# Two layers of graph attention on one core: gather indices, padding and score halves are read from where they are kept, and the copies go

## The chip, the cores and the metric

The kernel runs on one core of one Trainium2 chip. The metric is device time of that core in microseconds. The median of three runs of the kernel before is 1991.99 us (1989.11 to 1997.27). The engines are named as the profile names them: PE (matrix products), DVE (vector), ACT (activations), POOL (here the issuer of the row gathers) and SP (the issuer of the plain transfers).

## The reference

The input is x, 8192 nodes by 128 features, and adj, a matrix of 8192 by 8192 int32 in which about 9 entries a row are set. Two layers follow each other.

```
h = relu(layernorm(x))
# layer 0: scores from two projections
h0 = h @ W;  e = leaky_relu((h0 @ a1)[:, None] + (h0 @ a2)[None, :], 0.2)
x  = x + elu(softmax(where(adj > 0, e, -9e15)) @ h0)
h = relu(layernorm(x))
# layer 1: scores from query and key
q, k, v = h @ Wq.T + bq, h @ Wk.T + bk, h @ Wv.T + bv
x  = x + elu(softmax(where(adj > 0, q @ k.T / sqrt(128), -9e15)) @ v)
```

Since so few entries of a row are set, the kernel lists each row's neighbours once, gathers their rows and computes softmax over these alone. If a list overflows, a whole other branch does the full computation; for these inputs it isn't taken.

## The kernel before, in words

The 8192 rows are 64 tiles of 128 rows, one row a partition. All engines run a fully unrolled pipeline; the order of work on each is the order in which it is written, and semaphores join them.

**Layer 0, `survey`.** Step t of the loop works on several tiles at once. SP has loaded 4 MB of adj for a tile in four quarters; ACT turns each quarter into a BF16 mask (L1180), PE packs the mask into words in PSUM by 16 products of 512 columns (L1358), DVE pulls the largest words out (L701, L756 to L763, `decode` in every second step) and so gets up to 24 neighbours a row: 6 regular ones in the row's own list, and 18 more ("over") that are dealt among 384 places, 3 chunks of 128. For tile t-3 `mark` (L790, L793) says which places are whose, PE deals the lists out to them (L1422), ACT copies the result to `owned_list` (L1229), and `pick` makes the nine columns of indices, the padding and the part of the scores that is the row's own. POOL then issues nine gathers for the tile, 128 rows of a table each (L574), one column of indices each. For tile t-6 `score0`, `maxima`, `below` compute the scores (L847, L849, L841, L854 to L858, L862), for tile t-7 the rows are weighed and summed (L868, L875, L878, PE L1405, L891) and `finish` writes X.

The loop that joins the engines in a step: DVE L862 (`below`, waits for PE's L1398), then `pick`, `finish` and L868 on DVE, then PE L1405, L1391 and L1422, then ACT L1229 and two more quarters of the mask, then PE's L1358, and the next L862.

**Layer 1, `attend`.** The lists are kept, one entry a tile: `idx_all` (indices), `slot_all`, `pad_all` (padding, BF16), `end_all`, `pre_all`. Step t: `publish` copies the next tile's indices from `idx_all` to `idx_now` (four buffers) and tells POOL by `idx_done` (L1106), `prepare` rebuilds `hot`, `mine` and copies the padding to F32 (L1112 to L1118), `score1` computes the products with the gathered rows (L1129, L1132, L1135), `add_slots` sums (L883, L886). POOL issues nine gathers a tile (L604). There are four buffers `Gt` of gathered rows, so the gathers of tile t wait until `total` (L891) has finished tile t-4.

What the change touches is `pick` (L810 to L834), `score0` (L847), `maxima` (L854, L856), `publish` (L1106), `prepare` (L1113) and POOL's two gather loops.

## Time and profile before

| what | us |
|---|---|
| median of three runs | 1991.99 |
| profiled execution, its own time | 2002.33 |
| its span | 2000.6 |
| DVE busy / POOL busy / PE busy | 1361.0 / 1204.1 / 1256.1 |
| ACT busy | 772.2 |
| stretch 200 to 1040 us: layer 0 in its regular pace | 840 |
| stretch 1100 to 1950 us: layer 1 | 850 |

"Busy" counts the time in which an engine executes something; instructions that follow each other closely overlap in the records, so an instruction's duration can be longer than the distance to the next one's start. "<-" names who ended a wait; "remote" is a release that the profile can't put down to an instruction.

### The profile page before, as it was taken

The page shows a single profiled execution, that of the slowest core. Times are in us where ns is not written, and L with a number is a line of the kernel's source. Part 1 is how long each engine was busy: PE and PEld are TensorE (multiplying, and loading weights), DVE is VectorE, ACT ScalarE, POOL GpSimd, SP SyncE. Part 2 cuts the span into 40 slices and gives each one's busy share as a digit, 9 for nine tenths or more (in the row PEclk, how much of TensorE's full clock was granted, in tenths as well). Part 3 has the DMA queues.
Part 4 walks back from the last instruction along what each step waited for, and adds up shares of the span by engine and source line. Part 5 has one row for each costly group of instructions (what it writes and reads, how often), then busy time and mean ns, then how long its engine had stood idle before and what let it go on. Part 6 is the DMA issues. An engine that isn't in the chain of part 4 may idle for free.

```text
span 2000.6 us, 21643 instructions
## 1 busy us (share of the span) xinstructions
PE 1256.1 (63%) x5314; PEld 974.4 (49%) x5362; DVE 1361.0 (68%) x5505; ACT 772.2 (39%) x1507; POOL 1204.1 (60%) x1206
## 2 busy tenths in 40 slices
PE   2756677666776767776654345676766475838466
PEld 1433444444444444544444345575665475738355
DVE  4565777777777777777776356786776485838467
ACT  2774566565666666565631111121111111201111
POOL 1345555555555555555565566777777777757773
PEclk9886776766667666676765556655555555555666
DMA  9788999999999999989822111222222222212121
GB/s 311 272 310 322 326 318 330 336 310 325 316 334 321 330 310 332 331 320 329 313 55 48 50 45 49 58 54 57 53 57 54 54 55 57 54 44 60 49 56 40
DMA packets 122251, 372.31 MB, mean 186 GB/s; under 512 B 34577, under 2 KB 67858, under 8 KB 89362
## 3 DMA queue, kind: packets, MB, share of 16 engines
q1 hardware_dynamic: 75458, 289.83, 39.5%
q0 software_dynamic: 38464, 81.08, 15.7%
q10 hardware_dynamic: 8208, 0.03, 0.2%
q8 instruction: 46, 0.75, 0.2%
q14 instruction: 75, 0.61, 0.1%
HBM read 358.12 MB, written 12.72 MB: 185 GB/s over the span
## 4 chain that ended last, share of the span: by engine, by line
DVE 50%; another core or an unknown queue 19%; issue 12%; PE 10%; ACT 4%; POOL 2%; DMA 1%; SPq 1%; DVEq 0%; ACTq 0%; POOLq 0%
DVE arena L875 5%; DVE arena L701 3%; DVE arena L760 3%; DVE arena L763 3%; DVE arena L886 3%; ACT arena L1180 3%; DVE arena L1135 2%; POOL arena L604 2%; DVE arena L793 2%; DVE arena L868 2%; DVE arena L883 2%; DVE arena L1129 2%; PE psum L1398 1%; PE psum L1405 1%
## 5 line engine op out<-in xcount | busy, mean ns | idle before, releaser
L574 POOL DMA_INDIRECT arena<-table,arena x576 | 549.7, 954 | 424.1 <-DVE arena L829 262.2
L604 POOL DMA_INDIRECT arena<-table,arena x576 | 626.1, 1087 | 238.6 <-issue 171.0
L1180 ACT ACTIVATE arena<-arena 128x2048 bf16<-128x2048 int32 x256 | 485.4, 1897 | 26.2 <-DMA arena<-in_adj_dram 26.0
L1405 PE MATMUL psum<-arena 128*128 128x131 f32 (+1 forms) x768 | 206.2, 439 | 398.8 <-DVE arena L868 251.3
L1358 PE MATMUL psum<-arena 128*128 128x512 bf16 x976 | 334.9, 488 | 102.1 <-ACT arena L1180 55.2
L1405 PEld LDWEIGHTS psum<-arena 128*128 128x128 f32 x768 | 172.0, 322 | 414.0 <-issue 413.5
L1358 PEld LDWEIGHTS psum<-arena 128*128 128x128 bf16 x1024 | 117.6, 125 | 273.5 <-issue 169.0
L1315 ACT ACTIVATE arena<-psum 128x384 f32<-128x384 f32 x64 | 31.5, 492 | 437.9 <-PE psum L1525 202.0
L862 DVE TENSOR_TENSOR arena<-arena,psum 128x3 f32<-128x3 f32 x128 | 19.6, 153 | 260.6 <-remote 196.0
L1391 PEld LDWEIGHTS psum<-arena 128*128 128x128 f32 x768 | 161.6, 303 | 28.4 <-issue 15.6
L1391 PE MATMUL psum<-arena 128*128 128x18 f32 x768 | 152.7, 334 | 25.7 <-issue 14.2
L1398 PEld LDWEIGHTS psum<-arena 128*128 128x128 f32 x768 | 143.6, 264 | 50.5 <-issue 26.6
L1398 PE MATMUL psum<-arena 128*128 128x1 f32 x768 | 132.8, 288 | 32.1 <-issue 16.9
L1229 ACT ACTIVATE arena<-psum 128x465 f32<-128x465 f32 x64 | 35.7, 558 | 282.3 <-PE psum L1422 154.6
L875 DVE SCALAR_TENSOR_TENSOR arena<-arena 128x131 f32<-128x131 f32 x384 | 130.6, 340 | 6.5 <-DVE arena L878 2.0
L1211 ACT ACTIVATE arena<-arena 128x3 f32<-128x3 f32 x128 | 26.2, 205 | 273.5 <-DVE arena L862 160.5
L1422 PE MATMUL psum<-arena 128*128 128x155 f32 x384 | 120.8, 486 | 2.9 <-issue 1.4
L1524 PE MATMUL psum<-arena 128*128 128x128 f32 x384 | 120.0, 415 | 1.0 <-DVE arena L1123 1.0
L1525 PE MATMUL psum<-arena 128*128 128x129 f32 x384 | 117.5, 406 | 0.0
L886 DVE TENSOR_REDUCE arena<-arena 128x129 f32<-128x903 f32 x64 | 111.9, 1748 | 2.2
L1535 PE MATMUL psum<-arena 128*128 128x128 f32 x128 | 44.5, 445 | 103.6 <-ACT arena L1322 80.3
L856 DVE TENSOR_TENSOR arena<-psum,arena 128x18 f32<-128x18 f32 x128 | 21.9, 171 | 124.8 <-remote 122.6
(201 smaller groups left out, 2396.2 us busy)
## 6 DMA issues: line engine op xcount, KB each, us to landing
arena<-in_adj_dram SPq DMA_DIRECT2D x256, 1024.0 KB
arena<-table,arena POOLq DMA_INDIRECT x1152
table<-arena POOLq DMA_DIRECT2D x32, 132.0 KB, 5.3
arena<-table SPq DMA_DIRECT2D x64, 66.0 KB
table<-arena SPq DMA_DIRECT2D x16, 256.0 KB
arena<-table SPq DMA_DIRECT2D x64, 64.0 KB
out_dram<-arena SPq DMA_DIRECT2D x16, 256.0 KB
arena<-in_x_dram SPq DMA_DIRECT2D x4, 0.5 KB, 12.1
```

What stands on the lines that cost most here:

```text
L574: pool.indirect_dma_start(Gt[:, v % GROUP, c + 1, :], None, table0, bass.IndirectOffsetOnAxis(idx_now[:, v % GROUP, c:c + 1], 0))\
L604: pool.indirect_dma_start(Gt[:, t % GROUP, c + 1, 0:D], None, table1, bass.IndirectOffsetOnAxis(idx_now[:, t % GROUP, c:c + 1], 0))\
L875: nc.vector.scalar_tensor_tensor(out=acc_sb[:, k, 0:width], in0=Gt[:, r, c, 0:width], scalar=p10[:, k, c:c + 1], in1=acc_sb[:, k, 0:width] ...
L886: nc.vector.tensor_reduce(acc_sb[:, k, 0:DE], slots.rearrange("p c d -> p d c"), AX.X, ALU.add).then_inc(chained, 1)
L1180: nc.scalar.activation(mask[:, k, q * QUARTER:(q + 1) * QUARTER], adj_sb[:, k, q, :], ACT.Relu, accum_out=sum_all[:, bass.ds(tile, 1), q:q ...
L1358: nc.tensor.matmul(V[k], shifted[:, s, :], mask[:, k, s * 512:(s + 1) * 512], start=(s == 0), stop=False)
L1391: last = nc.tensor.matmul(by_slot_ps[k], owned[:, r, c, :], slot_e[:, k, c, :], start=(c == 0), stop=(c == CHUNKS - 1))
L1398: last = nc.tensor.matmul(max_ps[k][:, c:c + 1], mine[:, r, c * P:(c + 1) * P], neg_max[:, k, :], start=True, stop=True)
L1405: last = nc.tensor.matmul(acc_ps[k][:, 0:width], weighted[:, c, :], Gt[:, r, OWN + c, 0:width], start=(c == 0), stop=(c == CHUNKS - 1))
L1422: last = nc.tensor.matmul(deal_ps[v % 2][:, c, :], mine[:, v % GROUP, c * P:(c + 1) * P], dealt[:, v % GROUP, :], start=True, stop=True)
L1524: nc.tensor.matmul(own_ps[m][:, c, :], mine_c, ident[:, :], start=True, stop=True)
L1525: last = nc.tensor.matmul(uq_ps[m][:, c, :], mine_c, u_row[:, j, P:], start=True, stop=True)
```

## The change

`pick` writes its indices straight into the tile's entry of `idx_all` and its padding straight into `pad_all`; the F32 copy of the padding (`pad`), the four-buffered `idx_now` and the ten scores' own half (`s1_10`) are no longer there. POOL's gathers of both layers read `idx_all`. In layer 1 POOL no longer waits for `idx_done`, and `publish` and the copy of the padding are gone. `maxima` adds the BF16 padding. `score0` adds the own half in two instructions in place of one: seven columns with the row's own value from `self_s1` as scalar, three with what was dealt in `owned_list`. A tile of layer 0 has four DVE instructions less in `pick` and one more in `score0`; a tile of layer 1 has two less.

```diff
@@ gpsimd, layer 0 and layer 1 @@
-                                            bass.IndirectOffsetOnAxis(idx_now[:, v % GROUP, c:c + 1], 0))\
+                                            bass.IndirectOffsetOnAxis(idx_all[:, v, c:c + 1], 0))\
...
                     pool.wait_ge(summed, T + t - 3)
-                    pool.wait_ge(idx_done, T + t + 1)
...
-                                                bass.IndirectOffsetOnAxis(idx_now[:, t % GROUP, c:c + 1], 0))\
+                                                bass.IndirectOffsetOnAxis(idx_all[:, t, c:c + 1], 0))\
@@ pick @@
-            PICK_STEPS = 10
+            PICK_STEPS = 6
...
-                nc.vector.tensor_copy(s1_10[:, b, OWN:ROWS], ps[:, :, DEALT - 1]).then_inc(pick_done, 1)
+                nc.vector.tensor_scalar(idx_all[:, v, 0:REGULAR], dealt[:, b, LISTED:over], 0.0, float(N), ALU.max, ALU.min)\
+                  .then_inc(pick_done, 1)
                 after(1)
...
-                nc.vector.tensor_scalar(idx_now[:, b, 0:REGULAR], dealt[:, b, LISTED:over], 0.0, float(N), ALU.max, ALU.min)\
-                  .then_inc(pick_done, 1)
                 after(3)
...
-                nc.vector.tensor_scalar(s1_10[:, b, 0:OWN], ones[:, 0:OWN], dealt[:, b, DEALT - 1:DEALT], None, ALU.mult)\
-                  .then_inc(pick_done, 1)
-                after(5)
-                nc.vector.tensor_reduce(node_q[:, :], picked[:, :, :], AX.X, ALU.add).then_inc(pick_done, 1)
-                nc.vector.tensor_scalar(pad[:, b, :], dealt[:, b, P:LISTED + SLOTS], 0.0, NEG, ALU.is_le, ALU.mult)\
-                  .then_inc(pick_done, 1)
-                after(7)
-                nc.vector.tensor_scalar(idx_now[:, b, REGULAR:], node_q[:, :], 0.0, float(N), ALU.max, ALU.min)\
-                  .then_inc(idx_done, 1)
                 nc.vector.tensor_scalar(pad_all[:, at, :], one(dealt[:, b, P:LISTED + SLOTS]), 0.0, NEG, ALU.is_le, ALU.mult)\
                   .then_inc(pick_done, 1)
-                dve.wait_ge(idx_done, v + 1)
-                nc.vector.tensor_copy(idx_all[:, at, :], idx_now[:, b:b + 1, :]).then_inc(pick_done, 1)
+                after(4)
+                nc.vector.tensor_reduce(node_q[:, :], picked[:, :, :], AX.X, ALU.add).then_inc(pick_done, 1)
+                after(6)
+                nc.vector.tensor_scalar(idx_all[:, v, REGULAR:], node_q[:, :], 0.0, float(N), ALU.max, ALU.min)\
+                  .then_inc(idx_done, 1)
@@ score0 @@
-                nc.vector.tensor_tensor(e10[:, :], Gt[:, r, :, D], s1_10[:, r, :], ALU.add).then_inc(e_done, 1)
-                dve.wait_ge(e_done, u + 1)
+                nc.vector.tensor_scalar(e10[:, 0:OWN], Gt[:, r, 0:OWN, D], self_s1[:, u, 1:2], None, ALU.add).then_inc(e_done, 1)
+                nc.vector.tensor_tensor(e10[:, OWN:ROWS], Gt[:, r, OWN:ROWS, D], owned_list[:, r, :, DEALT - 1], ALU.add)\
+                  .then_inc(e_done, 1)
+                dve.wait_ge(e_done, 2 * u + 2)
@@ maxima @@
-                nc.vector.tensor_tensor(S[:, k, 0:OWN], l10[:, k, 0:OWN], pad[:, r, 0:OWN], ALU.add).then_inc(s_done, 1)
+                nc.vector.tensor_tensor(S[:, k, 0:OWN], l10[:, k, 0:OWN], pad_all[:, tt % T, 0:OWN], ALU.add).then_inc(s_done, 1)
...
-                nc.vector.tensor_tensor(S[:, k, OWN:], by_slot_ps[k], pad[:, r, OWN:], ALU.add).then_inc(s_done, 1)
+                nc.vector.tensor_tensor(S[:, k, OWN:], by_slot_ps[k], pad_all[:, tt % T, OWN:], ALU.add).then_inc(s_done, 1)
@@ prepare, attend @@
-                def publish(t, b):
-
-                    nc.vector.tensor_copy(idx_now[:, b:b + 1, :], idx_all[:, bass.ds(t, 1), :]).then_inc(idx_done, 1)
...
-                    nc.vector.tensor_scalar(pad[:, b:b + 1, :], pad_all[:, at, :], 1.0, None, ALU.mult).then_inc(hot_done, 1)
```

On DVE, `pick` of one tile in layer 0 before, from `below` (L862) to `finish` (L900):

```order
L862 TENSOR_TENSOR arena<-arena,psum 128x3 [waits max_spread]
L810 TENSOR_TENSOR arena<-arena 128x3 [waits owned_done]
L812 COPY arena<-arena 128x3
L814 TENSOR_TENSOR arena<-arena 128x54 [waits pick_done]
L817 TENSOR_SCALAR arena<-arena 128x6
L820 TENSOR_TENSOR arena<-arena 128x54 [waits pick_done]
L822 TENSOR_SCALAR arena<-arena 128x7
L825 TENSOR_REDUCE arena<-arena 128x3 [waits pick_done]
L826 TENSOR_SCALAR arena<-arena 128x25
L829 TENSOR_SCALAR arena<-arena 128x3 [waits pick_done]
L831 TENSOR_SCALAR arena<-arena 128x25
L834 COPY arena<-arena 128x9 [waits idx_done]
```

And the same place of the changed kernel (its line numbers differ; L853 is `below`):

```order
L853 TENSOR_TENSOR arena<-arena,psum 128x3 [waits max_spread]
L806 TENSOR_TENSOR arena<-arena 128x3 [waits owned_done]
L808 TENSOR_SCALAR arena<-arena 128x6
L811 TENSOR_TENSOR arena<-arena 128x54 [waits pick_done]
L815 TENSOR_TENSOR arena<-arena 128x54 [waits pick_done]
L817 TENSOR_SCALAR arena<-arena 128x25
L820 TENSOR_REDUCE arena<-arena 128x3 [waits pick_done]
L822 TENSOR_SCALAR arena<-arena 128x3 [waits pick_done]
```

The copy of the dealt half, the own half, the F32 padding and the last copy are gone; the six regular indices stand where the first copy stood, and two instructions now follow directly the one that they wait for.

On DVE, a step of layer 1 before, from `total` (L891) to `weigh` (L868):

```order
L891 TENSOR_TENSOR arena<-psum,arena 128x129 [waits chained,acc_done]
L894 RECIPROCAL arena<-arena 128x1 [waits summed]
L1112 TENSOR_SCALAR arena<-arena 128x384 [waits mine_done]
L1113 TENSOR_SCALAR arena<-arena 128x25
L1114 TENSOR_TENSOR arena<-arena 128x54
L1118 SCALAR_TENSOR_TENSOR arena<-arena 128x384 [waits fe_done]
L862 TENSOR_TENSOR arena<-arena,psum 128x3 [waits max_spread]
L900 SCALAR_TENSOR_TENSOR arena<-arena 128x128 [waits post_done,x_done]
L903 SCALAR_TENSOR_TENSOR arena<-arena 128x128 [waits y_done]
L1106 COPY arena<-arena 128x9
L868 TENSOR_TENSOR arena<-arena 128x384 [waits owned_done,p_done]
```

And of the changed kernel:

```order
L882 TENSOR_TENSOR arena<-psum,arena 128x129 [waits chained,acc_done]
L885 RECIPROCAL arena<-arena 128x1 [waits summed]
L1099 TENSOR_SCALAR arena<-arena 128x384 [waits mine_done]
L1100 TENSOR_TENSOR arena<-arena 128x54
L1104 SCALAR_TENSOR_TENSOR arena<-arena 128x384 [waits fe_done]
L853 TENSOR_TENSOR arena<-arena,psum 128x3 [waits max_spread]
L891 SCALAR_TENSOR_TENSOR arena<-arena 128x128 [waits post_done,x_done]
L894 SCALAR_TENSOR_TENSOR arena<-arena 128x128 [waits y_done]
L859 TENSOR_TENSOR arena<-arena 128x384 [waits owned_done,p_done]
```

The copy of the padding between L1112 and L1114 is gone, and so is `publish` ahead of `weigh`.

## Rows read from the trace of the kernel before

**Rows 1.** The page, busy time of each engine.
```profile
PE 1256.1 (63%) x5314; PEld 974.4 (49%) x5362; DVE 1361.0 (68%) x5505; ACT 772.2 (39%) x1507; POOL 1204.1 (60%) x1206
```
**Rows 2.** Waits, 200 to 1040 us: us in total, times, longest.
```profile
DVE arena L862 <- remote: 99.4, 28, 4.6
...
POOL arena L574 <- DVE arena L829: 226.8, 54, 4.9
```
**Rows 3.** Waits, 1100 to 1950 us: us in total, times, longest.
```profile
DVE arena L856 <- remote: 114.1, 19, 15.8
DVE arena L862 <- remote: 96.7, 13, 20.0
...
POOL arena L604 <- DVE arena L891: 58.9, 14, 13.3
```
**Rows 4.** Timeline, DVE in layer 0: start, us, instruction.
```profile
598.29 0.16 DVE L862 TENSOR_TENSOR arena<-arena,psum 128x3 f32<-128x3 f32 x1 [4.52 <-remote]
598.36 0.16 DVE L810 TENSOR_TENSOR arena<-arena 128x3 f32<-128x3 f32 x1
598.44 0.16 DVE L812 COPY arena<-arena 128x3 f32<-128x3 f32 x1
598.55 0.21 DVE L814 TENSOR_TENSOR arena<-arena 128x54 f32<-128x54 f32 x1
...
598.80 0.22 DVE L820 TENSOR_TENSOR arena<-arena 128x54 f32<-128x54 f32 x1
...
599.31 0.17 DVE L829 TENSOR_SCALAR arena<-arena 128x3 uint32<-128x3 f32 x1
599.38 0.17 DVE L831 TENSOR_SCALAR arena<-arena 128x25 bf16<-128x25 f32 x1
...
599.60 0.29 DVE L900 SCALAR_TENSOR_TENSOR arena<-arena 128x128 f32<-128x128 f32 x1
...
601.92 0.17 DVE L847 TENSOR_TENSOR arena<-arena 128x10 f32<-128x10 f32 x1
602.12 0.17 DVE L849 SCALAR_TENSOR_TENSOR arena<-arena 128x10 f32<-128x10 f32 x1
```
**Rows 5.** Timeline, the loop through PE and ACT after the next steps.
```profile
613.86 0.14 DVE L862 TENSOR_TENSOR arena<-arena,psum 128x3 f32<-128x3 f32 x1
...
617.80 1.65 PE L1405 MATMUL psum<-arena 128*128 128x131 f32 x6 [3.81 <-DVE arena L868]
...
622.97 0.56 ACT L1229 ACTIVATE arena<-psum 128x465 f32<-128x465 f32 x1 [4.52 <-PE psum L1422]
...
628.82 0.16 DVE L862 TENSOR_TENSOR arena<-arena,psum 128x3 f32<-128x3 f32 x1 [3.32 <-remote]
```
**Rows 6.** Groups of DVE instructions: xcount, busy, mean ns.
```profile
L822 DVE TENSOR_SCALAR arena<-arena 128x7 f32<-128x7 f32 x64 | 14.4, 225 | 0.0
...
L1113 DVE TENSOR_SCALAR arena<-arena 128x25 f32<-128x25 bf16 x64 | 11.4, 178 | 0.0
L1106 DVE COPY arena<-arena 128x9 uint32<-128x9 uint32 x64 | 11.3, 178 | 0.0
L826 DVE TENSOR_SCALAR arena<-arena 128x25 f32<-128x25 f32 x64 | 11.3, 176 | 0.0
...
L834 DVE COPY arena<-arena 128x9 uint32<-128x9 uint32 x64 | 11.0, 172 | 0.5 <-DVE arena L829 0.5
```
**Rows 7.** The page, gathers of layer 1: busy, mean ns, idle before.
```profile
L604 POOL DMA_INDIRECT arena<-table,arena x576 | 626.1, 1087 | 238.6 <-issue 171.0
```
**Rows 8.** Timeline, a `publish`, the gather beside it and the one before.
```profile
1524.26 0.94 POOL L604 DMA_INDIRECT arena<-table,arena  x1 [0.30 <-issue]
1525.51 0.98 POOL L604 DMA_INDIRECT arena<-table,arena  x1 [0.30 <-issue]
...
1525.92 0.17 DVE L1106 COPY arena<-arena 128x9 uint32<-128x9 uint32 x1
1525.99 0.55 DVE L868 TENSOR_TENSOR arena<-arena 128x384 f32<-128x384 f32 x1
```

More of the change, by code:

```diff
@@ L124, in two_layer_graph_attention @@
         hot = place([GROUP, CHUNKS, OVER])
-        pad = place([GROUP, 1 + SLOTS])
-        idx_now = place([GROUP, ROWS - 1], U32)
         owned_list = place([GROUP, CHUNKS, DEALT])
@@ L190, in two_layer_graph_attention @@
         e10 = place([ROWS])
-        s1_10 = place([GROUP, ROWS])
         picked = place([CHUNKS, OVER])
@@ L1133, in score1 @@
                       .then_inc(e_done, 1)
-                    dve.wait_ge(e_done, T + 2 * u + 2)
+                    dve.wait_ge(e_done, 2 * T + 2 * u + 2)
                     nc.vector.tensor_reduce(l10[:, k, :], prod[:, :, :], AX.X, ALU.add).then_inc(score_done, 1)
@@ L1142, in attend @@
                         back, m = (b - 3) % GROUP, (b - 3) % 2
-                        if live(t, -1):
-                            publish(t + 1, (b + 1) % GROUP)
                         if live(t, 3):
@@ L1165, in _ @@
                 dve.wait_ge(dve_consts, DVE_CONSTS + 3)
-                publish(0, 0)
                 unrolled(attend, G + 1)
```

## The prediction

> **What bounds the kernel now.** I read the busy times first, then the waits of each engine in the two regular stretches, then the timeline of a few steps. No engine is full: DVE, the busiest, has 68% of the span [rows 1]. So the time is in the loops that join the engines, and a removed instruction is worth what it shortens the loop in which it stands.
>
> Layer 0 has a pace of two steps. DVE starts L862 at 598.29, 613.86 and 628.82 us: 15.57 us and then 14.96 us [rows 4, 5]. Ahead of the first and the third it had waited, 4.52 and 3.32 us; ahead of the second it hadn't [rows 4, 5]. So one step of a pair (with `decode`) is DVE's own length, and the other is closed by the way through L868, PE, ACT and PE's L1398: L862 at 613.86, PE L1405 at 617.80, ACT L1229 at 622.97, L862 at 628.82 [rows 5]. The waits of the whole stretch say the same: 28 waits of L862, 99.4 us, none over 4.6, in 28 pairs of steps [rows 2]. The release is called "remote", so what exactly ends that wait the profile doesn't say. POOL isn't in this loop: it waited 226.8 us for the indices in the same stretch [rows 2].
>
> Layer 1 is less plain. DVE waits 114.1 us before L856 and 96.7 before L862, 32 times, "remote" again [rows 3]; POOL has 626.1 us of gathers and 171.0 of gaps between them, together 797 us, and waits for DVE's L891 only 58.9 us, 856 with it [rows 3, 7]: that is the length of layer 1 (the stretch of 850 us and its edges). So POOL is nearly full there, and a faster DVE can give at most those 58.9 us unless it makes the gathers shorter.
>
> **The change, part by part.**
>
> *`pick`.* Four instructions go: the copy L812, the own half L822, one of the two paddings (L826, L831) and the copy L834. L812 lasts 0.16 us [rows 4], the others 225, 176 and 172 ns [rows 6], 0.73 us together. But they overlap with their neighbours: L810, L812, L814 start 0.08 and 0.11 us apart [rows 4], and most of the removed ones fill the time in which a dependent instruction waits for its input. From L810 to L900 it now takes 598.36 to 599.60, 1.24 us [rows 4]. What is left is a chain: L814, then L820, the sum, the last three indices. L814 to L820 takes 0.25 us with a filler between; L814's 0.21 and the 0.03 that a dependent instruction adds (L847 lasts 0.17 and L849 starts 0.20 later, with nothing between) give 0.24 without [rows 4]. So the fillers inside the chain go for nothing, and the chain ends at 0.95 us as before (L810 to L829, [rows 4]). What is saved is its tail: L831 and L834 between L829 and L900, 0.29 us now [rows 4], of which 0.08 stays as the distance of two neighbours. That is 0.21 us a tile. The gathers see their indices at the same time as before; POOL's slack of 226.8 us covers them in any case [rows 2].
>
> *`score0`.* One instruction becomes two. The second starts 0.08 us after the first by the nearest row (L810 to L812), and the wait of L849 is for the later one: 0.08 us a tile more. Its upper end is a full duration and the wait, 0.20 us (L847 to L849) [rows 4]. This stands behind L868, so it lengthens DVE's own step, and not the part from L862 to L868.
>
> *`maxima`* reads the padding in BF16 beside F32. No row has just that; the nearest is L1113 with a BF16 input, 178 ns, against L826 with F32, 176 [rows 6]. Nothing, between -0.01 and +0.01 us a tile.
>
> *Layer 1.* `publish` goes: L1106 to L868 is 0.07 us [rows 8], and L868 is what PE waits for, so it stands in every step's loop. The copy L1113 lasts 178 ns [rows 6] but costs a distance of 0.08, and behind it DVE often waits at L862 anyway: between 0 and 0.08 us, I take 0.02. POOL's wait for `idx_done` ended nothing: all its waits were for L891 [rows 3]; 0. The gather beside a `publish` took 0.98 us [rows 8], and I count at most 0.04 us a tile for it, since a neighbour in the same shadow (L868) may be the cause.
>
> **The sum.** In layer 0 a pair of steps saves 0.21 in the step closed through PE and ACT and 0.21 - 0.08 = 0.13 in the one that is DVE's own, 0.34 us. Of the 32 pairs some 30 run at the regular pace (28 stand in the stretch alone, [rows 2]): 10.2 us. The other ends: 30 x 0.13 = 3.9, less the upper price of `score0` (0.12 more a tile, 7 us), so -3 us at worst; and 37 us if full durations counted (below). In layer 1, 64 x 0.09 = 5.8 us on DVE. Since POOL is nearly full, I take the half that its waits let through and a little for shorter gathers: 3.4 us; the ends are 0 and 64 x (0.15 + 0.04) = 12. Together 13.6 us. The profiled execution took 2002.33 us, 1.7 more than its span and 10.3 above the median; 2002.33 - 13.6 = 1988.7, which is 0.68% less, and on the median 1991.99 that is 1978.5. I say 1979.
>
> **Rules weighed.** The distances in rows 4 say that a small instruction costs 0.07 to 0.13 us where nothing waits on it. The Trainium skill ("VectorE: DVE Perf Modes", section "The TRN2 errata") says instead that instructions reading SBUF pay a fixed extra latency each, exposed between instructions. By that rule each removed instruction gives its whole length back, which is rival C; the starts 0.08 us apart speak against it.
>
> The gather beside a copy took 0.98 us, the one before it, with no copy beside it, 0.94 [rows 8]. The Trainium skill ("SBUF — State Buffer", section "Who interferes with whom") says that a copy or `tensor_scalar` in a 2-port mode takes a port pair that DVE shares with GpSimd and shuts it out for the whole instruction. By that rule POOL would win each removed copy in full, which is rival D.
>
> **The rivals.**
>
> B, hidden (chance 0.27): what ends the "remote" wait ahead of L862 isn't fed by L868 but by ACT's masks, whose pace is that of the adj loads. Then L868's earlier start ends in a longer wait, and only the DVE-owned steps shorten: 30 x 0.13 = 3.9 us, and layer 1, kept by POOL, gives 2. For it: the release has no name, and ACT reads the next quarters in the same loop. Against it: ACT L1229 waited 4.52 us for PE [rows 5], so ACT had time. Time: 1992 - 6 = 1986.
>
> C, full durations (0.03): 0.73 - 0.15 (L810's kind for the new one) = 0.58 us a tile, 37 us in layer 0, and 64 x (0.178 + 0.178) = 23 in layer 1: 1932.
>
> D, gathers set free (0.06): in layer 1 the two removed copies gave POOL back 0.178 us each a tile, 23 us there, with the 10 of layer 0: 1959. For it: POOL is the fuller engine there. Against it: a publish lasts 0.17 and the gather beside it grew by 0.04.
>
> E, slower (0.09): layer 1's "remote" stalls. They are 32 with 210.8 us, 6.6 us each [rows 3], and come after runs of short steps, when DVE has gained on POOL. A shorter DVE step can make such a run end sooner and bring another stall. Three more would cost 20 us against the 13.6 gained, +6; from three it decides, and with four it is +13: 2005. For it: layer 1's steps aren't regular, so small shifts are passed on. Against it: the sum of the stalls should stay what POOL's pace leaves over.
>
> **How the numbers follow.** My own case has the remaining 0.55, with a range of 1972 to 1986 (the ends of `score0` and of layer 1). Within 0.5% is about what a measurement of this kernel can't tell from no change; that is 1982 to 2002. About three quarters of my case lie below 1982, 0.42, with C and D 0.51, and a little of B: 0.53 faster. Same: the rest of my case, most of B and a third of E: 0.39. Slower: 0.08. The range of 8 in 10 reaches from 1964, halfway to D, to 1994, over B and up to where E begins.
>
> **What would show it.** In the profile after: L810's successor to L900's, 1.03 us instead of 1.24; the two steps of a pair at 15.44 and 14.75 us in place of 15.57 and 14.96; the waits of L862 in layer 0 nearly as long as now. If the 14.96 stays and the wait of L862 grows by 0.2 us each, B is right. If the step falls by over 0.5 us, C. In layer 1 the mean gather is to stay at 1.08 us or so; under 1.05 is D. POOL's wait for `total` should fall by a few us. The stalls before `maxima`'s second part and `below` should sum to about 200 us; over 230 is E. I am wrong if layer 0's stretch doesn't shorten by 7 us or more.

## The result: 4.3% slower, and where the time went

The changed kernel took 2069.57 us (median of 4 runs, 2062.02 to 2085.15) against 1990.55 beside it (4 runs, 1987.24 to 1997.27): ratio 1.0428, 95% interval 1.0388 to 1.0468 (the two medians alone give 1.040). The forecast was 1979. Ratios in this document are of fast runs: a run over 1.5% above the fastest of its kernel is left out of them, though not of the medians. The profiled execution took 2072.7 us, its span is 2071.0.

The page's busy times, with the columns of [rows 1]:
```profile
PE 1246.6 (60%) x5362; PEld 968.4 (47%) x5362; DVE 1335.0 (64%) x5185; ACT 773.2 (37%) x1507; POOL 1202.9 (58%) x1206
```
DVE has 320 instructions and 26 us less, and the span is 70.4 us longer. From the first `below` to the 64th (L862 before, L853 now) layer 0 took 940.2 us and takes 1014.8; layer 1 took 840.2 and takes 845.5. So the loss is in layer 0. The waits of its regular stretch, 200 to 1040 us, which answer [rows 2] (us in total, times, longest; POOL is GpSimd):
```profile
POOL arena L571 <- DVE arena L822: 240.6, 39, 14.7
...
DVE arena L780 <- remote: 97.0, 10, 11.1
...
DVE arena L853 <- remote: 58.8, 26, 4.4
...
DVE arena L780 <- issue: 19.8, 2, 9.9
```
A wait is there that before hardly had: DVE before L780, the first instruction of `split`, 12 times with 117 us (its counterpart L784 waited 2.8 us in all). `split` waits for PE's `ends` matmul, which is last of its step on PE. The starts of L853 show the pattern: groups of 14.8, 14.8, 12.1 and 24.7 us (66.4) where before had mostly 15.0 and 15.6 in turn (60.2 to 61.4 for four, 60.9 in the mean of 13 groups). In the two groups without a long step they are 14.8, 14.9, 14.8, 15.5: 60.0 us.

One long step on DVE, with start and duration, the wait ahead of it in brackets:
```profile
567.47 0.17 DVE L822 TENSOR_SCALAR arena<-arena 128x3 uint32<-128x3 f32 x1
567.55 0.29 DVE L891 SCALAR_TENSOR_TENSOR arena<-arena 128x128 f32<-128x128 f32 x1
...
570.71 0.56 DVE L859 TENSOR_TENSOR arena<-arena 128x384 f32<-128x384 f32 x1
581.16 0.16 DVE L780 TENSOR_TENSOR arena<-psum,arena 128x2 f32<-128x2 f32 x1 [9.89 <-issue]
```
On PE the same time reads as if the step's last matmuls had been done by 568.2:
```profile
564.12 0.72 PE L1381 MATMUL psum<-arena 128*128 128x1 f32 x6
...
567.66 0.39 PE L1348 MATMUL psum<-arena 1*128 1x512 bf16 x1
567.98 0.18 PE L1426 MATMUL psum<-arena 128*128 128x2 bf16 x1
571.48 1.65 PE L1388 MATMUL psum<-arena 128*128 128x131 f32 x6 [3.33 <-DVE arena L859]
582.33 1.47 PE L1374 MATMUL psum<-arena 128*128 128x18 f32 x6 [9.19 <-DVE arena L830]
```
The ends of matmuls are modelled. The semaphore events in the same trace are not, and they say otherwise: L1348's signal (`packed`) came at 580.43, 12.4 us after its recorded end, and L1388's at 581.92, not 573.1. GpSimd meanwhile ran two tiles' gathers through, with 0.79 us between them where 4 us are usual:
```profile
566.69 0.94 POOL L571 DMA_INDIRECT arena<-table,arena  x1 [0.30 <-issue]
568.43 0.95 POOL L571 DMA_INDIRECT arena<-table,arena  x1 [0.79 <-issue]
...
578.64 0.94 POOL L571 DMA_INDIRECT arena<-table,arena  x1 [0.30 <-issue]
```
From here on I read each PE signal by its lag, the semaphore event less the recorded end. I call a signal with a long lag held. Some events are missing from a trace, and such a signal then shows the next one's; a lag of about a step's length or more is such a case. Lags of `spread_max` (PE L1398 before, L1381 now), the signal that `below` waits for, from 200 to 1040 us:

| kernel | signals | lag under 0.3 us | 0.3 to 2 | over 2 |
|---|---|---|---|---|
| before | 55 | 0 | 0 | 55 |
| after | 50 | 12 | 9 | 29 |

Of the 21 early ones of the changed kernel, 10 came while their tile's gathers still ran, and the other 11, with 0.01 us, are those of the long steps, after the hold.

And in the trace of before, 53 of the 55 signals came 1.6 to 2.2 us (median 2.0) after the end of GpSimd's last gather of the tile, whatever PE had done by then. Here is one, GpSimd, then DVE:
```profile
564.75 0.94 POOL L574 DMA_INDIRECT arena<-table,arena  x1 [0.30 <-issue]
569.77 0.94 POOL L574 DMA_INDIRECT arena<-table,arena  x1 [4.08 <-DVE arena L829]
```
```profile
567.78 0.16 DVE L862 TENSOR_TENSOR arena<-arena,psum 128x3 f32<-128x3 f32 x1 [2.77 <-remote]
```
Last gather ends 565.69, signal 567.76, L862 at 567.78, next gather 569.77. That was the loop of the kernel before: nine gathers (8 x 1.25 + 0.94 = 10.95 us), 2.0 us to PE's signal, 2.0 us over `below` and `pick` to the next gather, 15.0 us. The "remote" of [rows 2] and [rows 5] was GpSimd going quiet.

Was PE's work held, or only its signals? The trace of before tells. Behind `spread_max` PE has eight wide products (L1358), L1364 and L1365, whose signal is `packed`:
```profile
392.85 0.72 PE L1398 MATMUL psum<-arena 128*128 128x1 f32 x6
393.43 1.02 PE L1358 MATMUL psum<-arena 128*128 128x512 bf16 x4
395.99 1.04 PE L1358 MATMUL psum<-arena 128*128 128x512 bf16 x4 [1.53 <-issue]
...
397.01 0.38 PE L1365 MATMUL psum<-arena 1*128 1x512 bf16 x1
```
The signal of L1398 came at 399.11 and that of L1365 at 399.22. Ten matmuls, 2.4 us by the records, can't have run in these 0.11 us. Both signals were late in 29 steps of the stretch, and in 28 of them they came 0.11 to 0.14 us apart. So PE had gone on computing, and its signals were held and came together at the end. In the long step shown above L1388's signal is 1.5 us behind `packed`; in others of the changed kernel it is 0.11 (447.62 and 447.73), with six matmuls of 1.65 us between.

### The profile page after: what moved, and what is told of

Read it like the earlier page. It is cut to its first block, busy times and chain, and to the rows that moved or that the text cites. A ratio compares the mean times of both kernels' runs of the same rounds, so it can differ in the third digit from the quotient of the medians.

```text
span 2071.0 us, 21308 instructions
## 1 busy us (share of the span) xinstructions
PE 1246.6 (60%) x5362; PEld 968.4 (47%) x5362; DVE 1335.0 (64%) x5185; ACT 773.2 (37%) x1507; POOL 1202.9 (58%) x1206
## 3 DMA queue, kind: packets, MB, share of 16 engines
q0 software_dynamic: 38464, 81.08, 14.9%
## 4 chain that ended last, share of the span: by engine, by line
DVE 46%; another core or an unknown queue 21%; POOL 12%; issue 10%; PE 5%; DMA 2%; ACT 2%; SPq 1%; DVEq 0%; ACTq 0%
POOL arena L600 12%; DVE arena L866 5%; DVE arena L877 3%; DVE arena L697 3%; DVE arena L1121 2%; DVE arena L756 2%; DVE arena L759 2%; DVE arena L859 2%; DVE arena L789 2%; DVE arena L1115 2%; DVE arena L874 2%; PE psum L1341 2%; ACT arena L1163 1%; DVE arena L891 1%
## 5 line engine op out<-in xcount | busy, mean ns | idle before, releaser
L600 POOL DMA_INDIRECT arena<-table,arena x576 | 618.9, 1074 | 238.9 <-issue 185.5
L1388 PE MATMUL psum<-arena 128*128 128x131 f32 (+1 forms) x768 | 199.5, 428 | 401.9 <-DVE arena L859 263.4
L1388 PEld LDWEIGHTS psum<-arena 128*128 128x128 f32 x768 | 165.9, 312 | 415.0 <-issue 413.0
L1374 PE MATMUL psum<-arena 128*128 128x18 f32 x768 | 158.0, 341 | 146.9 <-DVE arena L830 93.0
L1374 PEld LDWEIGHTS psum<-arena 128*128 128x128 f32 x768 | 162.0, 305 | 156.8 <-DVE arena L830 97.6
L1381 PEld LDWEIGHTS psum<-arena 128*128 128x128 f32 x768 | 146.7, 269 | 61.5 <-DVE arena L849 28.1
L853 DVE TENSOR_TENSOR arena<-arena,psum 128x3 f32<-128x3 f32 x128 | 19.9, 156 | 221.1 <-remote 149.9
L1381 PE MATMUL psum<-arena 128*128 128x1 f32 x768 | 135.3, 291 | 41.5 <-DVE arena L849 24.2
L1507 PE MATMUL psum<-arena 128*128 128x128 f32 x384 | 120.0, 415 | 1.0 <-DVE arena L1109 0.5
L697 DVE MAX8 arena<-psum 128x8 f32<-128x64 f32 x512 | 106.4, 225 | 0.3 <-PE psum L1348 0.3
L1507 PEld LDWEIGHTS psum<-arena 128*128 128x128 f32 x384 | 103.8, 330 | 1.4 <-issue 1.4
## 6 DMA issues: line engine op xcount, KB each, us to landing
arena<-in_x_dram SPq DMA_DIRECT2D x4, 0.5 KB, 12.1
```

The costliest lines, as they stand in the source:

```text
L600: pool.indirect_dma_start(Gt[:, t % GROUP, c + 1, 0:D], None, table1, bass.IndirectOffsetOnAxis(idx_all[:, t, c:c + 1], 0))\
L697: ins = nc.vector.max(words[:, b // 2, b % 2, 8 * n:8 * n + 8], V[b % 2][:, PLACE * n:PLACE * (n + 1)])
L1374: last = nc.tensor.matmul(by_slot_ps[k], owned[:, r, c, :], slot_e[:, k, c, :], start=(c == 0), stop=(c == CHUNKS - 1))
L1381: last = nc.tensor.matmul(max_ps[k][:, c:c + 1], mine[:, r, c * P:(c + 1) * P], neg_max[:, k, :], start=True, stop=True)
L1388: last = nc.tensor.matmul(acc_ps[k][:, 0:width], weighted[:, c, :], Gt[:, r, OWN + c, 0:width], start=(c == 0), stop=(c == CHUNKS - 1))
L1507: nc.tensor.matmul(own_ps[m][:, c, :], mine_c, ident[:, :], start=True, stop=True)
```

## The experiments

All ratios are to the kernel before, run on the same chip between the runs of the experiment; I call such a set of runs a session. Sessions fell into two conditions that I didn't choose: in some the kernel before takes 1765 to 1775 us, in others 1980 to 2028, as in the first pair. It isn't the chip alone: one chip gave 2008.85 for e12 to e14 and 1770.65 for e15 and e16. I call them "in time" and "late", after what PE's signals do.

**e1, e13: one wait more on GpSimd.** Edit, in the changed kernel:
```
 pool.wait_ge(idx_done, v + 1)
+pool.wait_ge(packed, min(T, v + PICK + 2))
```


> The changed kernel with one wait more on GpSimd in layer 0: before the ten gathers of tile v it also waits for `packed` of the step in which the pick of v runs (PE's last pack matmul of that step). In the changed kernel's trace that signal is there 1 to 2 us before the gathers start in a normal step, so the wait costs nothing there, and only in the long steps (24.7 us instead of 14.8, every fourth) do the gathers of the next tile (568.43 to 579.58 in the one looked at) start right behind those of the tile before (last one 566.69) and run through the whole time in which PE's pack_end, recorded at 567.66, has not signalled (580.43). Theory 'gathers run on': without GpSimd's run of 20 gathers in a row PE's signal comes within about 3 us of its recorded matmul, the long steps become about 15 us, layer 0 about 950 to 960 us, total about 1995 to 2010. Rival 'phase of PE and DMA': the held signal has nothing to do with the gathers; the long steps stay, the gathers of their tile start some 10 us later, and the total is 2070 or more.

In time: 1770.93 against 1772.83, ratio 0.9995 [0.9984, 1.0006]. It told nothing of the theory; it showed that 1990 isn't the only time of the kernel before.

**e2, e3, e4: parts and addresses.** e2: `pick` writes `idx_all` directly, its copy goes. e3: the new `score0` and `maxima` and three instructions fewer in `pick`. e4: the dropped buffers keep their places.
```
-nc.vector.tensor_copy(idx_all[:, at, :], idx_now[:, b:b + 1, :])       # e2
-nc.vector.tensor_tensor(e10[:, :], Gt[:, r, :, D], s1_10[:, r, :], ALU.add)   # e3
+nc.vector.tensor_scalar(e10[:, 0:OWN], Gt[:, r, 0:OWN, D], self_s1[:, u, 1:2], None, ALU.add)
+nc.vector.tensor_tensor(e10[:, OWN:ROWS], Gt[:, r, OWN:ROWS, D], owned_list[:, r, :, DEALT - 1], ALU.add)
+place([GROUP, 1 + SLOTS]); place([GROUP, ROWS - 1], U32); place([GROUP, ROWS])    # e4
```


> The kernel before with one part of the change: in layer 0 pick writes the indices straight into idx_all and the copy after it is gone, gathers of layer 0 read idx_all; the six small instructions that stand between the chain's steps stay, scores and pads as before, and layer 1 as before (it publishes and gathers from idx_now). Theory 'earlier in the step': what counts is how much DVE's pick shortens; this saves about 0.07 us a tile behind the gathers' signal, and I expect 1985 to 1995. Rival 'gathers from the list': if reading the indices from idx_all made the held signals, steps of about 25 us show and the time is over 2040.

> The kernel before with the other part of the layer-0 change: score0 takes its own half by a tensor_scalar and the owned half from owned_list (two instructions for one), maxima takes pad_all, and the three fillers that made s1_10 and pad are gone from pick; idx_now, its copy into idx_all and all of layer 1 stay. Theory 'gathers run on' or 'phase': pick up to the indices is barely shorter, so the tail saving is about 0.07 us and score0 0.1 us longer; if the long steps come from the score part (GpSimd's gathers set later or earlier against PE's pack), the time is over 2040 with steps of 25 us every fourth tile, else 1980 to 1995. No theory of mine puts it between 2000 and 2035.

> The changed kernel with the three dropped buffers (pad, idx_now, s1_10) still given their places and unused, so that every later tile in SBUF stands at the address it had before. If the addresses made the long steps (everything behind `hot` had moved by 544 bytes), the time falls to 1975 to 1995. If not, as both of my theories on time and order have it, 2060 to 2085 as for the changed kernel.

One run each, in time: 1771.97, 1772.79 and 1767.56 us beside 1772.83. Inconclusive, all three: the condition removed the effect that they were to divide. The idea of the addresses had its only test here and stays untested in the late condition.

**e5, e6: both kernels again, unchanged.**

> The changed kernel, word for word. On the chip of the first four experiments the kernel before took 1772.8 us and not 1991, with steps of about 12.5 us in layer 0 and 12.4 in layer 1. Theory 'held signals belong to the conditions of the first measurement': on a chip where PE's signals come with its matmuls the change is within 1% of before (1765 to 1780), no step of layer 0 is over 20 us but one, and the loss of 75 us needs the conditions of the first pair. Rival 'order': the change itself costs 4% on any chip, and this run is 1830 or more against 1773.

> The kernel before, word for word, for its trace on this chip. Both theories: within 0.3% of the runs of before beside it. What is asked is whether the waits of DVE for `below` and ACT's and DVE's late releases by PE (100 us in layer 0, 210 in layer 1 in the first trace) are there: by the theory of conditions they are under 40 us in all if the total is near 1773, and as before if it is near 1990.

e5: 1770.39 against 1770.68, ratio 1.0000 [0.9985, 1.0014]. So in this condition the change costs nothing and brings nothing that a measurement shows. e6: 1773.54, and in its trace all 295 PE signals between 200 and 900 us have a lag of 0.01 us, also the 192 that end at full clock beside a gather. DVE still waits 58.0 us for `below` from 200 us on, more than the 40 expected, but never over 7.6 and with PE's L1398 named as the releaser. The stretch, before (first trace) and e6 (us, then PE, PEld, DVE, ACT, POOL busy, the granted clock, DMA share, GB/s):
```profile
200.00:900.00 700.00, 490.13 (x1920) 319.44 (x1953) 521.99 (x2824) 438.98 (x663) 393.30 (x415) 0.69 0.92 324
```
```profile
200.00:900.00 700.00, 509.28 (x2238) 316.82 (x2276) 614.75 (x3317) 501.80 (x770) 469.00 (x491) 0.77 0.97 368
```
In time layer 0 fills the DMA engines to 0.97 at 368 GB/s; there I read the DMA engines as the bound, and a shorter `pick` has nothing to win.

**e7: layer 1's part alone.**
```
-pool.wait_ge(idx_done, T + t + 1)
-bass.IndirectOffsetOnAxis(idx_now[:, t % GROUP, c:c + 1], 0)
+bass.IndirectOffsetOnAxis(idx_all[:, t, c:c + 1], 0)
-publish(t + 1, (b + 1) % GROUP)
```


> The kernel before with only the part of the change in layer 1: no publish, gathers and maxima of layer 1 read idx_all and pad_all, no pad copy in prepare; layer 0 word for word as before. Theory 'held signals': where PE's signals come with their matmuls (before at 1773) this is within 5 us of before; where they come late (before at 1990) layer 0 keeps its steps of 15.0 and 15.6 us, none of 25, and the time is 1985 to 2000, since the +75 us sits in layer 0. Rival 'the list': under late signals the time is over 2030 though layer 0 is untouched.

In time again: 1769.88 beside 1773.66, one run each; within 5 us, as expected, and silent on the late condition.

**e8, e9, e10: PE's signals made later.** e8 on before, e9 on after, e10 is e9 with a hold every fourth step.
```
-for c in range(CHUNKS):
+for c in list(range(CHUNKS)) * (1 if tt >= T else 4):     # spread_max, layer 0
+if b == 2 and 6 <= t < T:                                   # e10, ahead of pack_end
+    pe.wait_ge(count_done, 3 * (t // 2))
+    for _ in range(56): nc.tensor.matmul(ends_ps, upto[:, :], over16[:, :], start=True, stop=True)
```


> The kernel before with PE's signal of spread_max made late on purpose in layer 0: its six matmuls run four times over before the signal, 18 more, which by the 0.83 to 1.83 us that six take in the trace of e6 is 2.5 to 5.5 us (in the first trace of before the signal came 3.6 us late in the median of 52). Theory 'held signals': this alone brings layer 0, 787 us here, most of the way to the 940 us of the first measurement, since below and pick stand behind it on DVE and ACT's last mask quarter and so SP's loads behind them: 14.3 to 16 us a step, total 1870 to 1960. Rival: layer 0 is bound by the DMA engines here (share 0.99) and has room for it: under 1800.

> The same 18 matmuls more in each step of layer 0 of the changed kernel. Theory 'the loss is the long holds alone': with an even delay in each step the shorter pick shows as I had forecast, about 0.1 to 0.3 us a step, so 5 to 20 us below e8. Rival 'the order turns any delay into a loss': 30 us or more above e8, with short and long steps in turn as in the first trace of the changed kernel.

> e9 and in every fourth step (b = 2, where the first trace of the changed kernel had its long holds) 56 small matmuls more on PE before pack_end, some 0.1 to 0.2 us each, so 6 to 11 us in which PE signals nothing (the trace had 12 to 14 us in ten steps). Theory 'long holds': such a step gets 6 to 10 us longer and no other gives it back, since DVE's split, ACT's next quarter and SP's loads all stand behind it: 14 to 15 such steps, total 75 to 150 us above e9. Rival 'given back': the buffers take it, under 40 us above e9, and then the long steps of the first trace were a sign and not the cause.

Late: before beside them 1999.28. e8 2027.63, ratio 1.0106 [1.0044, 1.0168]; e9 2021.03, 1.0093 [1.0051, 1.0134]; e10 2068.99 (one run). e8's total was forecast from 1773 and can't be judged. Its trace can: 18 more matmuls, and the median lag falls from 3.6 to 1.8 us: they end later, and the signal comes as before, in all 53 late ones 1.7 to 2.2 us after the last gather. That again fits a held signal and not held work. e9's total is 6.6 us under e8's, which their intervals don't part, and its layer 0 952.2 against 957.6 us, with no step over 16.2 us: with `spread_max` always behind the gathers the long steps are gone and the rival (30 us or more above e8) is wrong. e10 is 48 us over e9, between what the two theories gave (75 or more, under 40), but it can't judge them, for it didn't do what it was made for: the 56 matmuls took 1.5 to 2.1 us in 13 of the 15 steps and 3.2 and 4.1 in two, not 6 to 11. Eight steps are long even so (18.6 to 25.1 us). In eight of the 15 steps GpSimd began the next tile's gathers 0.19 us or more before the last of the 56 ended by the records; there `packed` has a lag of 1.5 to 11.2 us, and seven of these steps are 19.8 to 25.1 us long. In the other seven the gathers began within 0.11 us of that end or after it, and the lag is 0.01. One of each kind, PE and then GpSimd:
```profile
549.84 1.40 PE L1419 MATMUL psum<-arena 128*128 128x2 bf16 x50 [0.43 <-issue]
...
739.77 1.59 PE L1419 MATMUL psum<-arena 128*128 128x2 bf16 x56
```
```profile
552.01 0.94 POOL L571 DMA_INDIRECT arena<-table,arena  x1 [3.91 <-DVE arena L822]
...
740.83 0.94 POOL L571 DMA_INDIRECT arena<-table,arena  x1 [4.17 <-DVE arena L822]
```
In the first `packed` has no lag, in the second 4.8 us. So the long steps of e10 too are signals held beside gathers.

**e11: more load on PE.**
```
+for n in range(13 if s == 0 else 1):
     nc.tensor.matmul(V[k], shifted[:, s, :], mask[:, k, s * 512:(s + 1) * 512], start=(s == 0),
+                     stop=(s == 0 and n < 12))
```


> The kernel before with the first pack matmul of every tile (128x512) run 12 times more: 3 to 5 us more of wide matmuls a step, so PE busy nearly all of layer 0 beside DMA engines at a share of 0.9 or more. Theory 'load makes the holds': signals of PE later than the recorded end by more than 1 us appear in layer 0, as in the first trace (there up to 18 us). Rival 'the chip's own condition': they stay at 0.01 us on this chip whatever the load, and the step is only as long as the added matmuls make it, 14 to 16 us.

Late: 2009.01, one run, beside 1999.28. Layer 0 took 937.0 us where before's took 940.2, with twelve wide matmuls a tile more (643 us of PE busy against 580 from 200 to 1040 us). Its first step is 14.5 us and before's 23.3, though; without the first steps it is 922.5 against 916.9. The median lag is 1.8 us, not more than e8's. Load did not lengthen the hold, but as the session was late already, whether load starts it isn't told apart.

**e12, e13, e14: the decisive comparison, late.** e12 is the changed kernel, e13 is e1's kernel, e14 is e3's.

> The changed kernel, word for word, once more, as the measure for the two beside it. The time of the kernel before beside it tells the kind of chip: about 1773 (PE's signals come with its matmuls, e6: 0.01 us) or about 1990 (they come late, as in the first traces and in e8). Theory 'held signals': at 1773 no difference, as in e5; at 1990 the changed kernel is 2030 to 2085, with steps of 20 us or more every fourth tile of layer 0. Rival 'that one chip': at 1990 it is within 1% of before, since e9 had no long step in layer 0.

> As e1: the changed kernel, GpSimd's gathers of layer 0 also wait for `packed` of the step of their pick. If before is at 1990: theory 'gathers run on' expects no long steps, 1985 to 2000. Rival 'clock, DMA and PE's place in the step': the hold starts before the gathers of the next tile do (in the trace of the changed kernel PE's last signal in time is at 566.36 and the gathers start at 568.43), so the long steps stay and the time is 2060 or more. If before is at 1773, both expect no difference.

> As e3: the kernel before with the new scores and maxima alone (three small instructions less in pick, one more in score0), its copies of the indices kept. If before is at 1990: pick up to the indices is here 0.0 to 0.15 us shorter than before, half of the change's step; theory 'a place in the step is passed' expects long steps in some groups only or in none, 1985 to 2040; if it takes the whole loss (2060 or more), the scores are its cause and not the indices. If before is at 1773, no difference.

| kernel | us (median) | ratio to before, 2008.85 | layer 0, 1st to 64th `below` | steps over 20 us in it |
|---|---|---|---|---|
| e12 changed | 2049.75 | 1.0139 [1.0076, 1.0203] | 986.9 | 8 |
| e13 changed + wait | 1999.14 | 0.9963 [0.9929, 0.9997] | 928.2 | 0 |
| e14 scores only | 2020.39 | 1.0060 [1.0022, 1.0099] | 950.8 | 1 (the first) |

The long steps come back in another session, in fewer groups (8, where the first trace has 14), and cost less. The wait takes them away, and with them 50.6 us by the medians, 35 by the ratios: "gathers run on" was right, and its rival, that the hold begins before the gathers of the next tile and so doesn't need them, was wrong. The hold does begin before; the gathers keep it up. With the wait the largest lag of `packed` between 200 and 1040 us is 4.0 us (14.1 in e12). A held signal in e13, PE and then GpSimd:
```profile
566.10 0.39 PE L1349 MATMUL psum<-arena 1*128 1x512 bf16 x1
```
```profile
567.63 0.95 POOL L572 DMA_INDIRECT arena<-table,arena  x1 [0.31 <-issue]
571.89 0.95 POOL L572 DMA_INDIRECT arena<-table,arena  x1 [3.32 <-DVE arena L823]
```
The last gather ends at 568.58, `packed` comes at 570.5, and only then may the next gather start. In e12 GpSimd started the next tile 0.83 us behind the last, and DVE waited:
```profile
731.93 0.94 POOL L571 DMA_INDIRECT arena<-table,arena  x1 [0.30 <-issue]
733.71 0.95 POOL L571 DMA_INDIRECT arena<-table,arena  x1 [0.83 <-issue]
```
```profile
747.37 0.16 DVE L780 TENSOR_TENSOR arena<-psum,arena 128x2 f32<-128x2 f32 x1 [9.25 <-remote]
```
The traces without the added wait agree. From 200 to 1040 us a next tile's gathers start less than 1 us behind the last 12 times in the changed kernel and 6 in e12. Each time `packed` is held over 10 us (once its event is missing); before, e14 and e9 have no such start, and no lag of `packed` there over 3 us (one event of e14's is missing).

e14 has no long step after the first and all but one of its 55 `spread_max` signals have a lag over 2 us, as before: the scores alone don't set them off. It is 0.6% slower than before; its layer 0 is 10.6 us over the first trace's, from another session, so I leave that.

**e15 to e18: taking the gathers out, and using the loop.** e15 and e17 are e13 with `pick` ahead of `below` on DVE:
```
+if live(t, PICK):
+    pick(v, v % GROUP)
 if live(t, LATE):
     below(u, u % 2)
-if live(t, PICK):
-    pick(v, v % GROUP)
```
e16 and e18 are the kernel before with plain copies for gathers; they leave out the indices, so their rows and output aren't the reference's:
```
-pool.indirect_dma_start(Gt[:, v % GROUP, c + 1, :], None, table0,
-                        bass.IndirectOffsetOnAxis(idx_now[:, v % GROUP, c:c + 1], 0))
+pool.dma_start(Gt[:, v % GROUP, c + 1, :], table0[v * P + 1:v * P + 1 + P, :])
```


> e13 (the changed kernel, GpSimd's gathers of layer 0 behind `packed` of their step) with DVE's pick put in front of below, so that the indices are ready while PE's signal is awaited. In e13 and before a step of 15.0 us on a chip with late signals is nine gathers (8 times 1.25 us and 0.95, so 10.95), 2.0 us from the last one's end to PE's signal, and 2.0 us from that signal over below and pick to the next gather. Theory 'PE is held while GpSimd gathers': the last 2.0 us fall to about 0.2 to 1, the steps of layer 0 to 13.2 to 14 us, the total to 1880 to 1950 where before is 1990 to 2010. Rival 'a ring of DMA and clock': the steps stay at 15 us, since the same bytes have to move at the same rate, 1990 to 2010. Where before is at 1773 both expect no difference beyond 1%.

> The kernel before with the nine gathers a tile of layer 0 replaced by nine plain DMA copies of 128 rows of the table each, on the same queue's engine, same bytes and same signal, but no indices (the rows are not those of the reference, so the output is not). Theory 'PE is held while GpSimd gathers': PE's signals come with their matmuls in layer 0 (lag 0.01 us, at most a few over 0.3), a step is 12 to 13.5 us and the total about 140 to 180 us under before, where before is near 2000. Rival 'full clock and busy DMA engines hold it': the lags of 2 to 4 us at spread_max stay and so do steps of 15 us. Where before is at 1773, under 1% of difference.

> As e15, whose chip had PE's signals in time (before 1771, ratio 0.9996) and could not tell. If before is near 2000 here: theory 'PE is held while GpSimd gathers': the way from PE's signal to the next gather falls from 2.0 us to about 0.2 to 1, the steps of layer 0 from 15.0 to 13.2 to 14 us, total 1880 to 1950. Rival 'a ring of DMA and clock': steps stay at 15 us, 1990 to 2010.

> As e16: nine plain DMA copies a tile instead of nine gathers in layer 0, same bytes, other rows. If before is near 2000 here: theory 'PE is held while GpSimd gathers': PE's signals of layer 0 come with their matmuls, steps of 12 to 13.5 us, 140 to 180 us under before. Rival 'full clock and busy DMA engines hold it': lags of 2 to 4 us at spread_max and steps of 15 us stay.

e15 and e16 ran in time: 1769.69 (ratio 0.9996 [0.9985, 1.0007]) and 1765.88 beside 1770.65.

e18, late, took 1840.71 beside 1986.48: 146 us less, within the 140 to 180 expected. Its layer 0 took 781.5 us, less than e6's 790.3, and none of its 300 PE signals there is later than 0.01 us; in layer 1 of the same execution, where the gathers are left as they were, DVE still waits 88.0 us for a "remote" release before `below`, up to 20.7 at a time. Same chip, same execution, same bytes to move: the hold of PE's signals needs GpSimd's gathers. What in a gather does it, GpSimd's own work (0.94 us of it, and 0.53 in the mean for a plain copy) or the scattered rows, isn't told apart. The stretches of e18 in layer 0 and 1, with the columns from above:
```profile
200.00:900.00 700.00, 514.79 (x2292) 313.41 (x2291) 609.56 (x3353) 503.72 (x777) 258.72 (x489) 0.78 0.97 370
1100.00:1700.00 600.00, 371.72 (x1733) 345.76 (x1733) 410.56 (x956) 91.56 (x362) 434.94 (x402) 0.58 0.22 54
```
The DMA engines are as full (0.97) and PE's clock higher (0.78) than in the first trace (0.92, 0.69), so the rival, full clock and busy DMA engines, falls.

e17, late, took 1953.39 beside 1986.48: ratio 0.980 [0.9748, 0.9852], faster than the kernel before beside it, yet 3 us outside the theory's range (and 37 under the rival's). Layer 0 took 901.4 us, 14.3 a step, not 13.2 to 14. What was in the way, GpSimd's waits from 200 to 1000 us:
```profile
POOL arena L572 <- DVE arena L823: 139.9, 38, 4.5
...
POOL arena L572 <- PE psum L1349: 50.5, 15, 6.0
```
In most tiles it still waits for the indices: `pick` has moved ahead of `below`, but behind `count` it is late itself, and the way from PE's signal to the next gather fell from 2.0 to 1.6 us in the median, not to 1. The loop agrees with the size: 10.95 + 1.9 + 1.6 = 14.4 us.

## Why the prediction was wrong

**The loop.** The step that failed is "POOL isn't in this loop: it waited 226.8 us for the indices in the same stretch [rows 2]", and with it "POOL's slack of 226.8 us covers them in any case". The 226.8 us were 54 gaps of 4.2 us, and in these gaps PE's held signals came through. By the view of waits such a gap was slack; by the signals it was what another engine's release depended on. I had written that the profile doesn't name what ends L862's wait, and then put the masks in its place (rival B) and not GpSimd. [Rows 5] and a timeline of GpSimd beside it held the answer: nearly each release of L862 stands 2.0 us behind a last gather.

**No rival held the loss.** E looked for stalls in layer 1, from the "remote" waits of [rows 3]; they stayed what they were. The waits after, which answer [rows 3]:
```profile
DVE arena L847 <- remote: 117.0, 12, 19.1
DVE arena L853 <- remote: 87.3, 12, 20.1
```
204.3 us where 210.8 stood and "about 200" was forecast. What E described, short steps that a stall ends, is the pattern that layer 0 then showed, but E named neither that layer nor the gathers as the cause. The chance of slower, 0.08, came mainly from that one place.

**The terms.** Those of the sum held where the long steps are absent. L810 to L900 was 1.24 us (1.22 to 1.24 in all but one step), its successors L806 and L891 stand 1.01 to 1.09 apart (1.03 forecast):
```profile
554.39 0.15 DVE L806 TENSOR_TENSOR arena<-arena 128x3 f32<-128x3 f32 x1
...
555.32 0.17 DVE L822 TENSOR_SCALAR arena<-arena 128x3 uint32<-128x3 f32 x1
555.40 0.29 DVE L891 SCALAR_TENSOR_TENSOR arena<-arena 128x128 f32<-128x128 f32 x1
```
The indices come 0.93 us after L806, as forecast (0.95). `score0` costs 0.12 us more (0.32 from its first instruction to L840, before 0.20), within its bounds:
```profile
556.89 0.22 DVE L836 TENSOR_SCALAR arena<-arena 128x7 f32<-128x7 f32 x1
557.02 0.15 DVE L837 TENSOR_TENSOR arena<-arena 128x3 f32<-128x3 f32 x1
557.21 0.17 DVE L840 SCALAR_TENSOR_TENSOR arena<-arena 128x10 f32<-128x10 f32 x1
```
A group of four undisturbed steps fell from 60.9 to 60.0 us, about 0.45 a pair where I had 0.34, but there are only two such groups. With the long steps removed, e13's layer 0 is 12.0 us shorter than in the first trace of before (10.2 forecast). That agrees by luck: 8.5 of the 12.0 are the first step (14.8 against 23.3), the rest is 3.5 us, the two are from different sessions, and e13 has a wait more. Its ratio, 0.9963 [0.9929, 0.9997], takes in the 0.993 forecast and almost no change too. So the local distances were right, and what they are worth in the total isn't confirmed by any run; the mistake was to add them up for a loop whose closing condition wasn't known. In time they are worth nothing measurable (e5, 1.0000).

**Layer 1.** Its gathers took 1074 ns in the mean, before 1087 [rows 7]:
```profile
L600 POOL DMA_INDIRECT arena<-table,arena x576 | 618.9, 1074 | 238.9 <-issue 185.5
```
About as forecast ("1.08 us or so"), and no sign of rival D. Most of the 13 ns is chance: over the late traces the mean is 1077 to 1092 ns in the five that keep both instructions and 1069 to 1081 in the six without them, 8 ns a gather between the averages. That is 0.07 us a tile of the 0.36 us of DVE time removed. The Trainium skill ("SBUF — State Buffer", section "Who interferes with whom") lets a copy or `tensor_scalar` in a 2-port mode block GpSimd for its whole length when it was issued first; the trace shows no such return here, and whether the removed two ran in that mode no row tells. The Trainium skill ("VectorE: DVE Perf Modes", section "The TRN2 errata") has a latency exposed between instructions; as rival C read it, with each instruction's whole length given back, it isn't borne out: starts stand 0.07 to 0.13 us apart again, at durations of 0.15 to 0.22. Layer 1's 5.3 us of loss, where 3.4 of gain was forecast, is within what its irregular steps differ by from execution to execution. Late, it took 840.2, 857.0 (e8), 850.3 (e11), 855.4 (e14) and 850.6 us (e18) with both instructions in place, 850.7 in the mean, and 845.5, 849.9 (e9), 843.1 (e10), 853.8 (e12), 849.4 (e13) and 834.0 (e17) without them, 845.9: a difference of the forecast's size, but smaller than either spread.

**What set the long steps off.** By its traces: in the kernel before every one of 55 `spread_max` signals was late, so each next `pick` stood behind the end of the gathers and GpSimd always had its gap. In the changed kernel 10 of 50 came while gathers still ran. Then `below` and `pick` were early, the indices of the next tile were ready as the last gather ended (567.64 and 567.63 in the step shown), GpSimd ran on, and `pack_end`, which stands behind `spread_max` on PE, had its signal held for a whole tile's gathers. Nothing made up for it: `split` on DVE, ACT's next mask quarter and, behind it, SP's loads waited for it. An estimate: 12 such waits in 840 us with 117 us, less 3 us for each short step ahead (36), are 81 us, and the layer lost 74.6. That the run of gathers is needed is shown by e13. Why a signal slips through in the changed kernel and not in before is not: PE's last matmul of `spread_max` stood 7.2 to 9.5 us behind the first gather in the steps that slipped and 8.0 to 10.1 in those that were held. e3 and e2 were to divide it and ran in time; e14 clears the scores. The rest, the indices' part, the moved addresses and layer 1's part, wasn't run late, so which of them opens the gap stays open.

## What to carry to other kernels

An engine's idle time is slack only if nobody's release depends on it; before counting it, put the end of its last instruction beside the start of every unexplained wait, over ten steps, and look for a fixed distance. Where the profile says "remote", compare the semaphore's event with the recorded end of the matmul that sends it: a lag says that the signal was held, which the busy columns hide. Whether the work was held too, the next signal tells: here it came 0.11 us later with 2.4 us of matmuls between, so it wasn't. And an edit worth half a per cent needs the kernel before in more than one session, since here the same edit measured 1.043, 1.014 and 1.000.

## What the runs showed of the hardware that I had not expected

- PE's signals can be held while GpSimd issues indirect DMAs, and PE computes on meanwhile (28 of 29 pairs of signals 0.11 to 0.14 us apart with ten matmuls between, in before). In the late condition, in the first trace of before from 200 to 1040 us, by the granted clock at the recorded end and whether a gather ran or had ended less than 1.9 us ago: at full clock beside gathers 99 of 104 signals were over 0.3 us late, at half clock beside gathers 38 of 120, without a gather 0 of 24; 55 further signals with a lag over 14.5 us, where the event is missing, are left out. In e18, where plain copies take the gathers' place, 0 of 300.
- They come about 2.0 us after the last gather's end (within 1.6 to 2.2 us in 53 of 55 in before, 53 of 55 in e14, 53 of 58 in e17). In the changed kernel's 12 long holds from 200 to 1040 us `packed` came 0.2 to 3.0 us after the second tile's last gather in ten, 2.1 us before it in one, and in one its event is missing.
- The condition changes between sessions, also on one chip: before took 2008.85 and 1770.65 us on the same one. In the second (e15) all but one of 932 lags are 0.01 us, that one 17.1, with the same gathers and a DMA share of 0.97. What it is, isn't shown.
- Matmuls that end before the held signal would have come cost little: with twelve 128x512 ones more a tile layer 0 was 5.6 us longer without its first step (922.5 against 916.9, in different sessions).
